# A new order for every step of the delta attention, by turns of one unit, with a semaphore for each producer

## The reference

```python
q, k, v = (silu(causal_conv4(x @ W.T)) for W in (Wq, Wk, Wv))
e = k @ Wsv.T - v                      # three statistics of e, k, v per token
beta, amp = sigmoid(mlp_b(stats)), mlp_a(stats)      # 3 -> 32 -> 1 each
g = -exp(A_log) * softplus(k / |k| * amp + dt_bias)  # a decay per channel
def step(S, (q, k, v, g, beta)):       # q, k normalised; S is 128 x 128
    S = S * exp(g); S = S + outer(k, (v - k @ S) * beta); return S, (q * scale) @ S
o = rmsnorm(o) * norm_w * sigmoid(x @ Wg1.T @ Wg2.T + bg2);  out = o @ Wo.T
```

## Time and profile before

| | |
|---|---|
| median of the three runs | 6105.31 us |
| profiled execution, first to last instruction | 6108.1 us |
| first matmul of the delta stage | 31.99 us |
| first and last copy of chunk 0 into St | 148.3 and 2584.9 us |
| last output matmul of the stage starts | 2669.99 us |
| PE, DVE, ACT, POOL busy between 500 and 2400 us | 1634.37, 1396.56, 1078.69, 1271.18 us |

### The profile page before, as it was taken

One profiled execution on the slowest core, in us unless ns is written; L12 is line 12 of the kernel. 1 busy time (PEld: TensorE's weight loads), 2 busy tenths in 40 slices (PEclk: granted clock), 3 DMA queues, 4 the chain that ended last, 5 costly groups with the idle time before them and its releaser, 6 DMA issues. The chain is left out here.

```text
span 6108.1 us, 162699 instructions
## 1 busy us (share of the span) xinstructions
PE 5563.4 (91%) x69266; PEld 3711.6 (61%) x69266; DVE 3399.1 (56%) x7451; ACT 2691.6 (44%) x5744; POOL 1937.6 (32%) x2352
## 2 busy tenths in 40 slices
PE   5888888888888888889999999899989899999999
PEld 3666656666665666656777776533336667767665
DVE  5677777777777777633444443386624444444322
ACT  4555555555555555513555553236651222222211
POOL 3666666666666666610000000110000011111000
PEclk7999999999999999979999999989999999999999
DMA  0000000000000000000000000000010112111100
GB/s 28 7 7 7 7 7 7 7 7 7 7 7 3 7 7 7 3 17 12 15 11 11 15 10 23 7 1 1 1 56 1 37 67 67 67 67 67 63 7 7
DMA packets 34317, 116.15 MB, mean 19 GB/s; under 512 B 4416, under 2 KB 9792, under 8 KB 33600
## 3 DMA queue, kind: packets, MB, share of 16 engines
q1 hardware_dynamic: 33600, 105.74, 5.1%
HBM read 103.63 MB, written 2.10 MB: 17 GB/s over the span
## 5 line engine op out<-in xcount | busy, mean ns | idle before, releaser
L666 POOL TENSOR_TENSOR d_kq<-d_kq,d_tot 128x512 f32<-128x512 f32 x448 | 558.6, 1247 | 788.1 <-PE d_lpd L312 635.2
L723 DVE SCALAR_TENSOR_TENSOR d_qkv<-d_fr,d_wts,d_qkv 128x509 f32<-128x509 f32 (+2 forms) x576 | 428.3, 744 | 81.7 <-ACT d_qkv L534 72.6
L301 PE MATMUL d_fr<-xnT,d_wts 128*128 128x512 f32 x768 | 404.0, 652 | 9.4 <-DMA d_wts<-in_headw 5.2
L1845 DVE TENSOR_REDUCE r_nm<-r_ps 128x2 f32<-128x1024 f32 x256 | 307.8, 1223 | 138.7 <-PE r_ps L1664 138.6
L1943 PE MATMUL e_pj<-xnT,e_wts 128*128 128x512 f32 x768 | 347.9, 602 | 13.9 <-DMA e_wts<-in_w3all 12.2
L1059 POOL TENSOR_TENSOR f1rstd<-f1var,mhalf 128x4 f32<-128x4 f32 x4 | 4.0, 1010 | 1090.1 <-DVE f1var L1084 1090.1
L1765 ACT ACTIVATE r_pT<-r_ps 128x512 f32<-128x512 f32 x512 | 274.9, 598 | 146.3 <-PE r_ps L1672 145.8
L667 POOL TENSOR_TENSOR d_kF<-d_kF,d_tot 128x256 f32<-128x256 f32 x448 | 316.8, 707 | 0.0
L1296 PEld LDWEIGHTS c_po<-c_pT,c_vt 128*128 128x128 f32 x2304 | 294.7, 191 | 21.0 <-ACT c_pT L1361 9.3
L1296 PE MATMUL c_po<-c_pT,c_vt 128*128 128x128 f32 x2304 | 301.9, 276 | 0.2
L1664 PE MATMUL r_ps<-r_kT,r_qT 32*128 32x512 f32 x1024 | 291.5, 690 | 2.7 <-DVE r_nm L1845 1.1
(11 more groups left out here) (437 smaller groups left out, 13527.8 us busy)
## 6 DMA issues: line engine op xcount, KB each, us to landing
e_wts<-in_w3all SPq DMA_DIRECT2D x64, 897.0 KB, 4.6
d_wts<-in_headw SPq DMA_DIRECT2D x16, 583.5 KB, 3.9
c_wqo<-in_wqo SPq DMA_DIRECT2D x32, 256.0 KB, 2.6
f3ws<-in_f3w SPq DMA_DIRECT2D x17, 384.0 KB, 8.0
f2ws<-in_f2s SPq DMA_DIRECT2D x16, 256.0 KB, 6.2
f2qs<-in_f2q SPq DMA_DIRECT2D x16, 256.0 KB, 7.4
f1ws<-in_f1w SPq DMA_DIRECT2D x8, 384.0 KB, 5.7
f0ws<-in_f0w SPq DMA_DIRECT2D x6, 384.0 KB, 5.4
```

The lines of the kernel that those rows point to most:

```text
L301: last = nc.tensor.matmul(fr[:, bank, :], w_of(u)[:, w0 + kd * P:w0 + (kd + 1) * P], T.xnT[:, kd, tok(u):tok(u) + GRP], start=(kd == 0), s ...
L666: nc.gpsimd.tensor_tensor(v, v, bc(bc(t_l[:, :, 0], 2, h), 1, 2), ALU.mult)
L723: step = nc.vector.scalar_tensor_tensor(into, fr[:, x // 2, 0:GRP - 3 + i], tap(u, x, i), into, ALU.mult, ALU.add)
L1845: nc.vector.tensor_reduce(nm[:, t % 2, half, 4 * j + i0:4 * j + i0 + 2], ps[:, row_pair(row - 1):row_pair(row - 1) + 2], AX, ALU.max).then ...
```

## The change

The slots go. Each stream becomes a loop over turns `t`, and `unit(t, off)` gives the unit of a step: every step of every stream has its own offset in units, and comes once a turn. The order inside a turn is new on all four engines. Each producer that somebody waits for has a semaphore of its own, counted in units (`p_mm[3]`, `s_ready[2]`), and many waits that another implies are left out. The operations are the same but for their place. POOL's `scale` is split in three: `scaled_kq` comes after `kF` and `kq`, and the products `tot` of a level are done at other places. The units' data flow and all buffers stay.

```diff
-SL = 7
-K_AT, V_AT, Q_AT, SILU_AT, VT_AT, STAT_AT, SUMS_AT, ROOT_AT = 0, 1, 2, 4, 5, 6, 7, 8
-def at(g, off):
-    u, r = divmod(g - off, SL)
-    return u if r == 0 and 0 <= u < NU0 else None
+def unit(t, off):
+    return t - off if 0 <= t - off < NU0 else None
...
-        SLOTS = SL * (NU0 - 1) + Y_AT + 3
+        TURNS = NU0 + 30
...
                         sp.wait_ge(tg_mm, last + 1)
-                        sp.wait_ge(ez_ready, last + 1)
+                        sp.wait_ge(mz_ready, last + 1)
+                        sp.wait_ge(conv_q[2], last + 1)
                         sp.wait_ge(wo_ready, h - 1)
```

POOL, one turn, and how `scale` is split:

```diff
+                    if (u := unit(t, 28)) is not None:
+                        scale_kq(u, 0).then_inc(scaled_kq[0], 1)
+                        pool.wait_ge(p_mm[1], u + 1)
+                        scale_kF(u, 1)
+                        scale_kq(u, 1).then_inc(scaled_kq[1], 1)
...
+                        pool.wait_ge(p_mm[3], u + 1)
+                        scale_kF(u, 3)
+                        ch.did(scale_tot(u, 3), "scaled_tot[3]", u)
+                        scale_kq(u, 3).then_inc(scaled_kq[3], 1)
```

More of the change, by code:

```diff
@@ L361, in _ @@
[L361 to L371, removed]
+                    if (u := unit(t, 29)) is not None:
+                        pe.wait_ge(s_ready[2], u + 1)
+                        nc.tensor.matmul(ca[:, 0:P], kq[:, u % 2, 0, ch_(3)], St[:, u % 2], start=True, stop=True).then_inc(w_mm[3], 1)
@@ new lines, in _ @@
+                    if (u := unit(t, 28)) is not None:
+                        pe.wait_ge(xs_ready[5], u + 1)
+                        in_blocks(2 * P, Tb(0), Xb, (0,), 1, 1)
+                        in_blocks(P, Xb, Tb(0), (0, 2), 1, 0).then_inc(y_mm[5], 1)
+                    if (u := unit(t, 29)) is not None:
+                        pe.wait_ge(kF_ready, min(u + 3, NU0))
+                        pe.wait_ge(osq_ready, u + 1)
+                        for j in range(NC):
+                            last = nc.tensor.matmul(fr[:, 2, j:j + 1], osq[:, ch_(j)], T.ones[:, 0:1], start=True, stop=True)
+                        last.then_inc(ss_mm, 1)
@@ L377, in _ @@
+                    if (u := unit(t, 27)) is not None:
                         if u >= 2:
@@ L383, in _ @@
                         last.then_inc(dg_mm, 1)
[L384 to L394, removed]
@@ L501, in _ @@
-                    if (u := at(g, OUT_AT)) is not None:
-                        pe.wait_ge(osq_ready, u + 1)
-                        pe.wait_ge(kF_ready, min(u + 3, NU0))
-                        pe.wait_ge(diag_ready, min(u + 2, NU0))
-                        if u:
-                            pe.wait_ge(y_read, u)
-                        for j in range(NC):
-                            last = nc.tensor.matmul(fr[:, 2, j:j + 1], osq[:, ch_(j)], T.ones[:, 0:1], start=True, stop=True)
-                        last.then_inc(ss_mm, 1)
@@ new lines, in _ @@
+                    if (u := unit(t, 28)) is not None:
+                        pe.wait_ge(dl_ready[0], u + 1)
+                        nc.tensor.matmul(ca[:, 0:P], khat[:, ch_(0)], Dl[:, ch_(0)], start=True, stop=True).then_inc(s_mm[0], 1)
+                    if (u := unit(t, 27)) is not None:
+                        pe.wait_ge(low0_ready, u + 1)
+                        in_blocks(0, low_b(0), eye_b, range(NB), 0, 0)
+                        pe.wait_ge(scaled_kq[0], u + 1)
+                        products(u, 1).then_inc(p_mm[1], 1)
@@ L523, in _ @@
+                    if (u := unit(t, 28)) is not None:
+                        pe.wait_ge(s_ready[1], u + 1)
+                        nc.tensor.matmul(ca[:, 0:P], kq[:, u % 2, 0, ch_(2)], St[:, u % 2], start=True, stop=True).then_inc(w_mm[2], 1)
             @block.scalar
@@ new lines, in _ @@
+                    if (u := unit(t, 27)) is not None:
+                        for r in range(NB):
+                            nc.scalar.activation(TT[band(r), u % 2].rearrange("p (c r i) -> p c r i", c=NC, r=NB)[:, :, r], c3(TB[band(r), 0]), ACT.Copy)
+                        act.wait_ge(x_mm[6], u + 1)
+                        nc.scalar.activation(Xs[64:, 0:256], xy[64:, 0:256], ACT.Copy).then_inc(xs_ready[6], 1)
+                    if (u := unit(t, 25)) is not None:
+                        if u % 4 == 0:
+                            nc.scalar.mul(negA[:, head(u) % 2], negA[:, head(u) % 2], -1.0)
@@ L643, in _ @@
+                    if (u := unit(t, 25)) is not None:
+                        act.wait_ge(ez_ready, u + 1)
+                        nc.scalar.activation(ezs[:, 2], ez[:], ACT.Square, bias=shift[:, 2:3])
             @block.gpsimd
@@ new lines, in _ @@
+                    if (u := unit(t, 26)) is not None:
+                        dve.wait_ge(ezs_ready[1], u + 1)
+                        ch.after("factor[0]", u)
+                        ch.did(factor(1), "factor[1]", u)
+                        ch.after("factor[1]", u)
+                        ch.did(factor(2), "factor[2]", u)
+                    if (u := unit(t, 23)) is not None:
+                        if not first(u):
+                            nc.vector.tensor_tensor(early[:, :, :, 2], tail[:, u % 2, :, 2:5], bc(taps(u)[:, :, 2], 2, 3), ALU.mult)
```

1095 lines of the change are left out of this document (600 added, 495 removed).

## The result

The changed kernel takes 5594.95 us (median of four runs, 5593.59 to 5602.62) where the kernel before takes 6099.65 (median of four): ratio 0.917, interval 0.914 to 0.919, so 505 us less. The profiled execution of after spans 5592.5 us. Single executions that ran slower (one of e3 with 5783.21 us, one of e6 with 9050.18, two of e16 with 17030.63 and 17227.08) are left out of all ratios.

A forecast was written before the change was run, and what follows sets the result against it. Bound by the order in which streams meet: a DVE and PE cycle of 33.3 us plus 1.7 of waits gives 35.0 against 39.94 us, 306 us less over 62 units, so 5800 us, range 5680 to 6020.

The forecast's parts named there:

- The allowance of 1.7 us: PE's waits: half of the earlier 3.4 us a unit would remain, raising the turn from 33.3 to 35.0 us.
- What is late next: PE at W1 and X1, waiting for DVE: 1 to 2 us idle, none over 2.00 us, so low clock goes.
- DVE's chain: DVE's queue from TB3 to TB at level 0: 19.7 us, 20.5 with waits inside it.
- PE's stretch: PE from X1 to Y3, after DVE's queue: 12.0 us of work, 0.4 for late ACT, 0.4 for hand-overs.
- PE alone: PE's own work at full clock: 32.8 us a unit, the lower bound of a turn.
- rival one: PE reaches its own limit, a turn of 33.0 us, 5675 us in all; chance 0.12.
- Semaphores and dropped waits: Synchronisation, judged from DVE's lp steps: between 0 and 0.1 us a unit either way, taken as 0.
- Levels and `tot`: POOL's chain with PE: all levels fit with 0 to 0.5 us to spare, `tot` (0.3 us) no longer in it.
- Head and end: Before the first St copy and the last 95 us: latency-bound, 3.4 turns at the head, equal within 20 us.
- Rival two: Clock still falls once a unit, idle gathering at W1 and X1: turn 38.5 us, 6016 us; chance 0.14.
- Rival four: The waits only move elsewhere: turn 39.9 us within 0.3, 6105 us; chance 0.06.
- Rival three: DVE and POOL hold one another up: turn 41.5 us, 6200 us; chance 0.08.

The follow-up runs named there:

- e3: Kernel after with the gate's matmul done twice, 0.9 us more PE per unit beside DVE's chain: 5660.26 us, ratio 0.926 to the kernel before.
- e6: Kernel before with `tot` alone taken out of POOL's chain with PE: 6122.51 us, ratio 1.001.
- e16: Kernel after once more, unchanged but for a space in a class line: ratio 0.9163 to the kernel before, 32.13 us a unit.
- e10: Kernel after with 26.3 already satisfied waits a unit added to PE's stream: 5705.22 us, ratio 0.933 to the kernel before.
- e14: Kernel before with 35.5 already satisfied waits a unit added to PE's stream: 6167.85 us, ratio 1.009.
- e7: Kernel after with `tot` of levels 0 to 4 put back into POOL's chain with PE: 5654.78 us, ratio 0.925 to the kernel before.
- e5: Kernel before with chunk 0's state written to St at the slot's beginning, ahead of convolutions and early columns: 6112.11 us, ratio 1.000.
- e12: Kernel after with DVE's addition x3 (0.5 us) moved out of the chain to behind the bar: 5605.72 us, ratio 0.917 to the kernel before.
- e11: Kernel after without three of the four matmuls summing the output's squares (0.66 us of PE): 5581.94 us, ratio 0.913 to the kernel before.
- e1: Kernel after with a spare 0.69 us DVE multiplication per unit inside DVE's chain: 5621.16 us, ratio 0.919 to the kernel before.
- e4: Kernel after with the `wsv` matmul done twice, 0.9 us in PE's stretch: 5627.23 us, ratio 0.921 to the kernel before.

## Why the prediction was wrong

The direction and most of the mechanism held: the clock is 1.00, the long stops for St and R are gone, and the cycle over DVE and PE closes in a turn, with PE as full as DVE's chain. The size was off, 7.95 us a unit and not 4.94, and 34 us in head and end that I had at zero. The forecast turn of 35.0 us was 3.0 too long: 1.7 of allowance against 0.2 measured, 20.5 of chain against 19.3, 12.8 of stretch against 12.5. By its steps:

- **The allowance of 1.7 us, half of the waits of the earlier trace rows.** The step that failed, and the largest miss. It was laid on top of a cycle in which I had already counted the waits one by one (0.8 + 0.4 + 0.4 us). Measured, chain and stretch leave 0.2 us of a turn, and PE stands for 0.8 in all. Of the four groups three are gone and Xs fell from 0.7 to 0.3 us a unit.
- **What is late next: 1 to 2 us of idle at W1 and X1, for DVE.** It did not come: neither is among PE's waits. The longest stop is one of 2.36 us beside a weight load, with no named cause: that a wait not named would be PE's longest was one of the prediction's own signs of being wrong.
- **DVE's chain, 20.5 us with its waits.** 19.3 measured in the turn shown, with 18.3 busy and 1.0 of waits, where I had 19.7 and 0.8. I had taken all of the 29.4 us of a unit as DVE's own work; in the kernel before, steps that lie in the chain were held up, as shown below (`hid3` and TB0), and a unit of DVE is now 28.1.
- **PE's stretch, 12.0 + 0.4 + 0.4.** Measured 12.5 in the turn shown, with one wait of 0.40 for Xs as forecast: right within 0.3.
- **PE alone, 32.8 us.** A whole turn, stops included, takes 31.99, and PE's busy time is 31.2. So as PE's work it was 1.6 us too high, and as a floor it stood 0.8 above what was reached; it made rival one look less likely than it was. The dropped waits explain little of it: e10's 26.3 waits bring PE's busy time only from 31.2 to 31.7, e14's 35.5 from 34.4 to 34.8, and part of that is clock. A record of PE holds the way through the array, and counts in full where it follows a stop. A record of a 128 x 128 matmul lasts 0.275 us, but adds only some 0.11 behind a neighbour (two span 0.39). The trace of before has 362 stops over 0.15 us between 500 and 2400 us, 7.6 a unit; after has 75 in 1500 us, 1.6 a unit. Six fewer at 0.16 are an estimated 1.0 of the 1.6 us: so much was not work. The rest stays open.
- **Semaphores and dropped waits, 0 with bounds of 0.1 us a unit.** Wrong by its source: the idle time between DVE's lp steps says nothing of PE, where 19.6 waits a unit went, at 0.02 to 0.055 us each by e14 and e10.
- **Levels and `tot`.** Right as far as is seen: PE waits for no level, and with `tot` put back it does, at two groups of them (e7, with the reservation made there). In the old order taking it out is worth nothing (e6).
- **SyncE, zero.** Nothing waits for the weights, but beside six of the loads PE stands, 11 us in sum, which I had not foreseen.
- **Head and end, equal within 20 us.** They gained 17 us each. The head, from first projection to first copy, is 116.3 us in before and 86.3 in after, 2.9 and 2.7 turns and not 3.4. So latency is nearly a fixed number of turns there, and the turn got shorter; this is read off the two traces, not tested.

Rival one (T = 33.0) was nearer than the forecast, and still too high by a microsecond. Rival two did not come: between 500 and 2000 us the clock falls behind two of the loads' stops, and not once a unit. Rival four is what e5 shows for one edit, and does not hold for the whole change.

Rival three did not come either, and here the rows show why. DVE's steps of one kind under POOL (busy, mean ns), to be held against the earlier trace rows:

```profile
L869 DVE SCALAR_TENSOR_TENSOR d_lp<-d_ez 128x512 f32<-128x512 f32 x47 | 65.8, 1401 | 0.0
L813 DVE TENSOR_SCALAR d_qkv<-d_qkv 128x512 f32<-128x512 f32 x47 | 32.2, 685 | 0.0
L839 DVE TENSOR_SCALAR d_qkv<-d_qkv 128x512 f32<-128x512 f32 x47 | 19.5, 415 | 0.0
L830 DVE TENSOR_SCALAR d_bx<-d_ba,d_mb 128x4 f32<-128x4 f32 x47 | 39.6, 843 | 0.0
L914 DVE SCALAR_TENSOR_TENSOR d_lp<-d_lp,d_mz 128x512 f32<-128x512 f32 x47 | 32.5, 692 | 3.0
```

Round q is back to 415 ns, round k now takes 685, the first lp step 1401, twice one of the earlier trace rows, and `bx`, which ACT waits for, 843 where the kernel before has 230. These three lose 1.6 us a unit, but all lie behind the bar, outside the chain. In the kernel before DVE lost 0.62 on round q, and inside the chain 0.37 on `hid3` (790 ns, now 417) and 0.24 on TB0 (523, now 284). The early columns had some too. So such losses are not gone; what changed is where they fall. POOL's scaling even got shorter, with a mean of 1176 where it was 1249 in the kernel before:

```profile
L700 POOL TENSOR_TENSOR d_kq<-d_kq,d_tot 128x512 f32<-128x512 f32 x328 | 385.7, 1176 | 29.9 <-PE d_lpd L324 29.9
```

By the exclusive lock of the Trainium skill ("SBUF — State Buffer", section "SBUF: two separate sides") the turn could not be under 34.2 us, as I had worked it out. It is 31.99 with POOL busy for 26.0 of it: as a floor made of all such DVE steps the rule does not hold here. The last lp step (L914 above) shows it most plainly: it reads two tiles in SBUF, POOL is busy from its start to its end in all 47 units, and it takes 692 ns. The three long steps show a loss of the kind; that POOL causes it is argued from their neighbours in time, no run parts it.

## What to carry to other kernels

When a walk through a new order has priced each meeting, add nothing on top for "waits that will be left": give the walk as the forecast and the busiest engine's own time as the lower end, and distrust that own time if it was read in a stream that stops often. Waits dropped from the fullest engine are worth counting, 0.02 us each on PE and up to 0.055 where they bring more "issue" stops. Twice here a stall that ends at a queue's order was not mended by moving one step (e5, e6). Once streams are tied, taking 0.5 or 0.66 us from one of them returned 0 to 0.2 us (e12, e11), and adding 0.69 to 0.9 cost from a third of it to all (e1 to e4).

## What was not expected of the hardware

In the kernel after, PE's stops without a named cause come only at every 256th record of its stream: 46 of 46, and 47 of 47 in e16. A weight load of 583.5 KB at 242 GB/s that is issued 0.3 to 0.7 us ahead of such a place goes with a stop of 1.5 to 2.4 us at the next (six of 14 loads, the same six in e16); in pieces of 146 KB the longest is 1.3 us.

A wait that is already satisfied costs PE 22 ns in a stream that is busy for 86% of the time (34.4 of 39.94 us) and 55 ns at 97%, of which all but 20 ns are such stops.

The stop of 1.81 us was followed by 7 us at a clock of 0.76, while the one of 2.36 us, ended at 967.02 us in the same trace, left it at 1.00, and so did the one of 2.00 us in the earlier trace rows: the length of one stop does not decide it.
